# Row sums from a column of ones, context normalised in rows, and a gated output matrix, in an attention and expert layer

## The chip, the cores and the metric

The kernel runs on one core of one Trainium2 chip. The metric is device microseconds of one execution; lower is better. The numbers come from timed runs and from one profiled execution, whose rows are shown below. The engines are PE (TensorE; PEld its weight loads), DVE (VectorE), ACT (ScalarE), POOL (GpSimd) and SP (SyncE, which issues most transfers).

## The reference

The input is x of 16 batches x 256 positions x 128 channels in fp32. Six vectors per batch (shift, scale and gate, for attention and for the feed-forward part) come from a small product. With LN for the layer norm:

```
h = LN(x) * (1 + ca) + sa
Q, K, V = h @ Wq + bq, h @ Wk + bk, h @ Wv + bv        # 16 heads of 8
scores = Q K^T / sqrt(8) + Q . rel_table[clip(j - i)]
ctx = softmax(scores) V
x = x + ga * (ctx @ Wo + bo)
h = LN(x) * (1 + cb) + sb
x = x + gb * mixture of the 2 best of 8 experts(h)
```

Two facts let the kernel treat parts of this apart. The softmax's denominator may be applied after the product with V. And the gate ga differs by batch and channel only, so ga * (ctx @ Wo + bo) is ctx @ (Wo with its columns scaled by ga) plus the row ga * bo.

## The kernel before, in words

The attention stage is a hand-written pipeline over steps. A step (b, p) treats pair p (0 to 7, called slot p below) of heads of batch b: 128 steps in all. Every engine has a program of its own, in which `step(b, p)` is written out in order, and engines meet through counting semaphores only. In a step

- DVE takes the maxima (line 1312): four passes of 128x256 add the bias to the scores in psS and store the negated scores in NS and their extremes in nmax. It then takes the result of a job from psM (lines 1214 to 1236), copies the distances of six steps ahead from psDist to `stage` (line 1267, `put_out`), and takes the result of an extra job (line 1242).
- ACT computes four exponentials from NS to P (line 711). Each also sums its row into lsum (`accum_out`), which the profile shows as a second instruction, ACTIVATION_READ_ACCUMULATOR. Then ACT copies the turned P of the step before from psT to PT (line 722, `gather`).
- PE does, in this order: extra jobs of the slot; turn, eight transposes of P of the step before (line 968); scores of the next step, interleaved with the distances of six steps ahead (lines 950 and 956); a part of weigh, the product of PT with V into psO (line 984); and a job of the slot into psM.
- SP stores `stage` to DRAM and reads it back as `bias`, skewed.
- POOL prepares Q and K, the second layer norm and the rows for the experts.

Two tables set which jobs lie in which slot. `M_SLOTS` are jobs in psM: q23, k01, k23 in slots 0 to 2, logits and v in slot 3, y and nh in slot 4, u01, u23 and q01 in slots 5 to 7, each with a shift in batches. `X_SLOTS` are extra jobs in a spare part of psDist: rank, turn, back, tally (last batch), rows, and t in slots 1 to 6. `W_SLOTS` says which group of weigh stands where: group 0, both halves, in slot 4, and the last half of group 3 in slot 2 of the next batch. So the context of batch b-1 is completed in slots 0 to 4 of batch b:

1. Slot 0, DVE: `inverses` (line 1316) waits for all exponentials of the batch and takes the reciprocals of the 32 sums per row.
2. POOL: `widen` (line 565) repeats each reciprocal 8 times into linvD.
3. Slot 2, PE: `spread_l` (line 991) transposes linvD into the right half of psO. The left half holds the context, with the channels in the partitions.
4. Slot 3, ACT: `sums` (line 739) copies that half to lrow. DVE: `context` (line 1322) multiplies psO by lrow into ctxT.
5. Slot 4, PE: y (line 865) multiplies WoD by ctxT into psM; ACT applies the gate and the gated bias into yT (line 730), and t (line 902, slot 6) transposes yT back; DVE adds it to X (line 1247).

The columns of V are spread so that head c of group g lies in columns of its own: 32 columns per weight load, of which 8 hold values. psO is overwritten by the next batch's group 0, so weigh waits there for `ctx_done` (line 977).

After the attention stage the remaining jobs are closed, and the experts run over 39 tiles of 256 rows, with PE as the engine that is busy throughout; at the end results are weighed and stored.

Before the first step SP issues the loads one after the other: Wo and bv in four pieces each, then the rest of X, then 2 MB of zeros to DRAM.

The code of the functions that the change touches, with the line numbers of the profile:

## Time and profile before

| | |
|---|---|
| three runs | 685.5, 687.17 (median), 690.84 us |
| profiled execution | 685.29 us, its span 683.6 us |
| first maxima to the end of the last (128 steps) | 30.1 to 483.0 us of the span |
| busy in the span | PE 588.5, PEld 439.8, DVE 507.1, ACT 508.8, POOL 423.3 us |
| granted clock, mean | 0.96 of 2.4 GHz |

How to read it: the span runs from the first instruction to the last. A row of a timeline has the start in the span, the duration, the engine, the line in the code, the operation, output<-inputs, and the shapes; a bracket at its end is idle time of the engine before it and what ended it. Instructions overlap their neighbours, so the distance between two starts is what the first one costs its engine, and is less than its duration. Matmul rows are merged where they follow each other; x8 is their count. Idle time of an engine that others do not wait for costs nothing.

### The profile page before, as it was taken

To read this page: it belongs to the slowest core of one execution; us is meant where nothing else is said; L and a number is where in the kernel's file an instruction comes from. 1 tells how busy PE (TensorE), PEld (TensorE's weight loads), DVE (VectorE), ACT (ScalarE), POOL (GpSimd) and SP (SyncE) were. 2 spreads that over 40 slices of the span, in tenths; PEclk is the share of its full clock that TensorE was granted. 3 is DMA by queue.
4 is the path that set the end of the run, shared out by engine and by line. 5 is a ranking of instruction groups with operands and counts; after the bars stand their busy time and mean duration, and the time that the engine had idled before them with its cause. 6 is when DMAs were issued, how large, how long until landed. Compare 5 with 4: busy or idle time off the path is not lost. (4 is left out here: it accounts for less than half of the span.)

```text
span 683.6 us, 17706 instructions
## 1 busy us (share of the span) xinstructions
PE 588.5 (86%) x5108; PEld 439.8 (64%) x5108; DVE 507.1 (74%) x1888; ACT 508.8 (74%) x1578; POOL 423.3 (62%) x543
## 2 busy tenths in 40 slices
PE   5667789999899899899989989978798989999950
PEld 4444556666666566566666656655577979999940
DVE  6788988999999999999999999997565312222127
ACT  4157799999999999999989999998643434444434
POOL 2660655747668687686776966855366765554535
PEclk9777999999999999999999999999999999999975
DMA  5996678778787788778868878874525777565538
GB/s 142 308 230 202 198 235 248 228 235 248 214 245 241 213 252 246 228 219 260 249 208 242 252 213 247 243 236 148 189 82 174 236 234 228 198 217 185 176 97 274
DMA packets 173125, 149.03 MB, mean 218 GB/s; under 512 B 16182, under 2 KB 162642, under 8 KB 173030
## 3 DMA queue, kind: packets, MB, share of 16 engines
q1 hardware_dynamic: 168054, 139.33, 67.9%
q0 software_dynamic: 4544, 8.44, 3.7%
q8 instruction: 43, 0.70, 0.4%
q14 instruction: 52, 0.43, 0.2%
q10 hardware_dynamic: 432, 0.14, 0.1%
HBM read 83.71 MB, written 65.05 MB: 218 GB/s over the span
## 5 line engine op out<-in xcount | busy, mean ns | idle before, releaser
L711 ACT ACTIVATE P<-NS,nmax 128x256 f32<-128x256 f32 x512 | 254.2, 504 | 50.5 <-DVE nmax L1312 49.6
L1312 DVE CUSTOM_DVE_ANT_0 NS<-psS,bias 128x256 f32<-128x256 f32 x512 | 185.2, 417 | 2.3 <-PE psS L950 1.6
L968 PE MATMUL psT<-ident,P 128*128 128x128 f32 x1024 | 140.0, 281 | 8.9 <-ACT PT L722 8.8
L1267 DVE COPY stage<-psDist 128x768 f32<-128x768 f32 x125 | 118.1, 945 | 33.9 <-issue 25.2
L722 ACT ACTIVATE PT<-psT 128x512 f32<-128x512 f32 x256 | 136.4, 586 | 0.0
L968 PEld LDWEIGHTS psT<-ident,P 128*128 128x128 f32 x1024 | 118.2, 145 | 24.0 <-issue 9.8
L778 ACT ACTIVATE F<-psS,b1T 128x256 f32<-128x256 f32 x156 | 65.4, 471 | 86.5 <-PE psS L1061 86.5
L609 POOL DMA_INDIRECT results_d<-y,row_u x78 | 76.0, 974 | 56.7 <-DVE y L1458 40.8
L711 ACT ACTIVATION_READ_ACCUMULATOR P<-NS,nmax 128x1 f32 x512 | 100.3, 196 | 0.0
L950 PE MATMUL psS<-Kst,Qst 32*128 32x256 f32 x512 | 65.9, 336 | 34.7 <-DVE nmax L1312 29.9
L1061 PE MATMUL psS<-xT,w 128*128 128x256 f32 x312 | 80.6, 381 | 0.3 <-DMA w<-in_L_ffn_w_dram 0.3
L587 POOL TENSOR_TENSOR th<-z,th 128x512 f32<-128x512 f32 x28 | 35.7, 1277 | 70.8 <-ACT th L737 70.8
L601 POOL DMA_INDIRECT slots_d<-rows,slot_u x64 | 63.1, 987 | 26.4 <-issue 16.9
L984 PE MATMUL psO<-PT,V 128*32 128x256 f32 x1024 | 79.3, 394 | 0.0
L950 PEld LDWEIGHTS psS<-Kst,Qst 32*128 32x128 f32 x512 | 39.1, 189 | 62.2 <-DVE nmax L1312 52.0
L887 PE MATMUL psM<-hT,Wqk 128*128 128x256 f32 x244 | 70.1, 411 | 1.1 <-DVE z L1226 1.0
L956 PE MATMUL psDist<-Tst,Qst 32*128 32x192 f32 x488 | 58.2, 317 | 0.0
L887 PEld LDWEIGHTS psM<-hT,Wqk 128*128 128x128 f32 x244 | 43.1, 196 | 23.1 <-DVE xqk L1234 6.9
L1061 PEld LDWEIGHTS psS<-xT,w 128*128 128x128 f32 x312 | 53.4, 191 | 5.6 <-issue 1.0
L1458 DVE TENSOR_TENSOR y<-psO,b2R 128x256 f32<-128x256 f32 x19 | 8.1, 424 | 52.5 <-PE psO L1071 45.4
L1458 DVE TENSOR_TENSOR y<-psT,b2R 128x256 f32<-128x256 f32 x20 | 8.5, 425 | 51.8 <-PE psT L1071 47.8
L519 POOL TENSOR_TENSOR part<-xqk,lowQ 128x512 fp32r<-128x512 f32 x32 | 33.3, 1041 | 21.9 <-DVE xqk L1234 15.5
(254 smaller groups left out, 1044.2 us busy)
## 6 DMA issues: line engine op xcount, KB each, us to landing
dist_d<-stage SPq DMA_DIRECT2D x128, 384.0 KB, 3.0
bias<-dist_d SPq DMA_DIRECT2D x256, 192.0 KB, 3.3
w<-in_L_ffn_w_dram SPq DMA_DIRECT2D x39, 512.0 KB, 3.7
x<-slots_d SPq DMA_DIRECT2D x39, 129.0 KB, 3.0
y<-results_d SPq DMA_DIRECT2D x16, 256.0 KB, 5.0
dist_d<-zeros SPq DMA_DIRECT2D x1, 2048.0 KB, 14.4
out_dram<-y SPq DMA_DIRECT2D x8, 256.0 KB, 3.2
results_d<-y,row_u POOLq DMA_INDIRECT x78, 3.0
```

Source lines behind the costliest of these rows:

```text
L601: pool.indirect_dma_start(out=slots_d, out_offset=bass.IndirectOffsetOnAxis(ap=slot_u[:, j, n:n + 1], axis=0), in_=rows[:, j, r % RINGS, k ...
L609: pool.indirect_dma_start(out=results_d, out_offset=bass.IndirectOffsetOnAxis(ap=row_u[:, j, k:k + 1], axis=0), in_=y[:, j % HELD, k, :], ...
L711: act.activation(P[:, p % 2, h, q, :], NS[:, p % 2, h, q, :], ACT.Exp, scale=-1.0, bias=nmax[:, p % 2, k:k + 1], accum_out=lsum[:, b % 2, ...
L722: act.activation(PT[:, (p // 2) % 2, 2 * (p % 2) + h, :], psT[:, h, :], ACT.Copy)\
L778: i = act.activation(F[:, j % 2, k, :], psH[:, half, ET * n:ET * n + ET], ACT.Silu, bias=b1T[:, bass.ds(which[j], 1), k:k + 1].rearrange(" ...
L887: mm = pe.matmul(bank[:, S * n:S * n + S], w[:, 128 * g:128 * g + 128], hT[:], start=True, stop=True)
L950: mm = pe.matmul(psS[:, h, S * q:S * q + S], Qst[at, b % 2, g, 128 * q:128 * q + 128], Kst[at, b % 2, g, :], start=True, stop=True)
L968: mm = pe.transpose(psT[:, h, S * k + 128 * q:S * k + 128 * q + 128], P[:, p % 2, h, q, 128 * k:128 * k + 128], ident[:])
L984: mm = pe.matmul(psO[32 * a:32 * a + 32, 0:S], V[:, par, k, g, a, :, :].rearrange("p c d -> p (c d)"), PT[:, g % 2, a, S * k:S * k + S], s ...
L1061: mm = pe.matmul(psH[:, half, ET * n:ET * n + ET], w[:, j % DEEP, 0, at], xT[:, j % 2, :], start=True, stop=True)
L1267: dve.tensor_copy(stage[:, p % STAGES, :, :, :], bank[:, :, 0:2 * RW].rearrange("p h (q c) -> p h q c", q=2)).then_inc(dist_out, 1)
L1312: dve.tensor_tensor_reduce(NS[:, p % 2, h, q, :], psS[:, h, S * q:S * q + S], bias[:, p, h, q, :], 1.0, 3e38, ALU.add, ALU.min, nmax[:, p ...
```

## The change

The exponentials no longer sum their rows. V gets 16 columns per head instead of 8: eight values, a column of ones (written once), and seven of zeros; group g fills one half of psO (`g // 2`), so that psO's 512 columns hold, for each of 16 heads, eight values and the sum. The context of batch b-1 then goes another way:

1. Slot 3, ACT: `copy_values` copies all of psO to C. PE: `turn_values` transposes C back into psO in four pieces, with the positions in the partitions.
2. Slot 4, DVE: `context` takes the reciprocals of the 32 sums per row from psO and multiplies the values by them into ctx_r.
3. Slot 4, PE: ct transposes ctx_r into psM; ACT copies it to ctxT.
4. Slot 6, PE: y multiplies with ctxT as the stationary operand by WoG, and adds a product of a repeated column of the identity with gR, which gives every row the gated bias of the batch. DVE adds it to X.
5. Slot 7: gain. PE repeats the batch's gate row, DVE multiplies Wo by it into WoG. In batch 0, slot 4, gains turns all gates and gated biases into gR.

`inverses`, `widen`, `spread_l`, `sums` and t go. Wo and bv are reordered on the host, so that each is one transfer.

```diff
-           (("y", -1), ("nh", 2)), (("u01", -2),), (("u23", -2),), (("q01", 2),))
-X_SLOTS = ((), (("rank", -4),), (("turn", -2),), (("back", -2),), (("tally", 1 - B),), (("rows", -3),), (("t", -1),), ())
+           (("ct", -1), ("nh", 2)), (("u01", -2),), (("u23", -2),), (("q01", 2),))
+X_SLOTS = ((), (("rank", -4),), (("turn", -2),), (("back", -2),), (("gains", 0), ("tally", 1 - B)), (("rows", -3),),
+           (("y", -1),), (("gain", 0),))
...
-        V = early("V", [128, 2, JB, HG, 4, HG, D])
+        V = early("V", [128, 2, JB, HG, 4, 2, 2 * D])
...
-            for a in range(4):
-                at = slice(32 * a, 32 * a + 32)
-                sp.dma_start(WoD[at, :], Wo.rearrange("(g a d) e -> a g d e", a=4, d=D)[a]).then_inc(weights_in, 16)
-                sp.dma_start(bvT[at, :], bv.rearrange("(g a d x) -> a g d x", a=4, d=D, x=1)[a],
-                             allow_slow_non_contiguous=True).then_inc(weights_in, 16)
+            sp.dma_start(WoD[:], Wo).then_inc(weights_in, 16)
+            sp.dma_start(bvT[:], bv.rearrange("(e a) -> e a", a=1)).then_inc(weights_in, 16)
...
-                if b > 0:
-                    widen(b - 1)
...
                     act.activation(P[:, p % 2, h, q, :], NS[:, p % 2, h, q, :], ACT.Exp, scale=-1.0,
-                                   bias=nmax[:, p % 2, k:k + 1],
-                                   accum_out=lsum[:, b % 2, q, a, p // 2:p // 2 + 1]).then_inc(exp_done, 1)
+                                   bias=nmax[:, p % 2, k:k + 1]).then_inc(exp_done, 1)
...
-                    i = act.activation(yT[:], bank[:, 0:S], ACT.Identity, scale=modT[:, 2, b:b + 1],
-                                       bias=gabo[:, b:b + 1])
+                    i = act.activation(ctxT[:], bank[:, 0:S], ACT.Copy)
...
-            def sums(b):
-                act.wait_ge(ctx_full, b + 1)
-                past(act, ctx_done, b)
-                act.activation(lrow[:], psO[:, S:2 * S], ACT.Copy).then_inc(lrow_done, 1)
+            def copy_values(b):
+                act.wait_ge(values_done, HG * b + HG)
+                past(act, ctx_full, b)
+                act.activation(C[:], psO[:], ACT.Copy).then_inc(c_copied, 1)
...
-                elif name == "y":
+                elif name == "ct":
                     pe.wait_ge(ctx_done, b + 1)
-                    mm = pe.matmul(bank[:, 0:S], WoD[:], ctxT[:], start=True, stop=True)
+                    for k in range(2):
+                        mm = pe.transpose(bank[:, 128 * k:128 * k + 128], ctx_r[:, k, :], ident[:])
...
-                elif name == "t":
-                    pe.wait_ge(m_act, M_TAKEN["y", r][1])
+                elif name == "y":
+                    pe.wait_ge(m_act, M_TAKEN["ct", r][1])
+                    pe.wait_ge(x_dve, X_TAKEN["gain", r][0])
                     for k in range(2):
-                        mm = pe.transpose(spare[:, k, :], yT[:, 128 * k:128 * k + 128], ident[:])
+                        pe.matmul(spare[:, k, :], ctxT[:, 128 * k:128 * k + 128], WoG[:], start=True, stop=False)
+                        mm = pe.matmul(spare[:, k, :], ident[:, r:r + 1].broadcast_to([128, 128]), gR[:, 1, :],
+                                       start=False, stop=True)
...
+                elif name == "gain":
+                    mm = pe.matmul(spare[:, 0, :], ident[:, r:r + 1].broadcast_to([128, 128]), gR[:, 0, :],
+                                   start=True, stop=True)
...
-                        mm = pe.matmul(psO[32 * a:32 * a + 32, 0:S],
+                        mm = pe.matmul(psO[32 * a:32 * a + 32, S * (g // 2):S * (g // 2) + S],
...
-            def spread_l(b):
-                pe.wait_ge(linv_wide, b + 1)
+            def turn_values(b):
+                pe.wait_ge(c_copied, b + 1)
                 for q in range(2):
-                    mm = pe.transpose(psO[:, S + 128 * q:S + 128 * q + 128],
-                                      linvD[:, q, :, :, :].rearrange("p a g d -> p (a g d)"), ident[:])
+                    for r in range(2):
+                        mm = pe.transpose(psO[:, S * q + 128 * r:S * q + 128 * r + 128],
+                                          C[:, S * r + 128 * q:S * r + 128 * q + 128], ident[:])
                 mm.then_inc(ctx_full, 1)
...
-                    if p == 2:
-                        spread_l(b - 1)
+                if p == 3 and b > 0:
+                    turn_values(b - 1)
...
+                elif name == "gain":
+                    i = dve.tensor_tensor(WoG[:], WoD[:], spare[:, 0, :], ALU.mult)
...
+                values = psO[:].rearrange("p (n m d) -> p n m d", n=4, d=2 * D)
+                dve.wait_ge(ctx_full, b + 1)
+                dve.reciprocal(linv[:], values[:, :, :, D:D + 1].rearrange("p n m d -> p n (m d)")).then_inc(linv_done, 1)
                 if b > 0:
-                    dve.wait_ge(m_full, M_FULL["y", b - 1])
-                dve.tensor_tensor(ctxT[:], psO[:, 0:S], lrow[:], ALU.mult).then_inc(ctx_done, 1)
+                    dve.wait_ge(m_full, M_FULL["ct", b - 1])
+                dve.wait_ge(linv_done, b + 1)
+                dve.tensor_tensor(ctx_r[:].rearrange("p q (r m d) -> p (q r) m d", r=2, d=D), values[:, :, :, 0:D],
+                                  rep(linv[:], 3, D), ALU.mult).then_inc(ctx_done, 1)
...
-                if p == 0 and b > 0:
-                    inverses(b - 1)
...
-                if p == 3 and b > 0:
+                if p == 4 and b > 0:
                     context(b - 1)
```

What stands in a row on DVE in slot 4 of a batch, between the maxima of two slots (ISA rows are the maxima; the list counts lines of the changed kernel a little differently). Before:

```order
L1312 ISA nmax 128x1
L1229 TENSOR_SCALAR logitT<-psM,rb2T 128x256
L1222 COPY V<-psM 128x2x4x8 x4
L1267 COPY stage<-psDist 128x768
L1312 ISA NS,nmax<-psS,bias 128x256
```

With the change:

```order
L1316 ISA nmax 128x1
L1225 TENSOR_SCALAR logitT<-psM,rb2T 128x256
L1218 COPY V<-psM 128x2x4x8 x4
L1323 RECIPROCAL linv<-psO 128x32
L1327 TENSOR_TENSOR ctx_r<-psO,linv 128x256
L1268 COPY stage<-psDist 128x768
L1316 ISA NS,nmax<-psS,bias 128x256
```

The reciprocals and the context's product now stand between the copies of V and the copy to `stage`; before, they stood in slots 0 and 3.

What stands in a row on PE in slots 3 and 4 of a batch, from scores of slot 3 to turn of slot 5's extra jobs. Before:

```order
L881 MATMUL psM<-z,rw_s 32x256 x4
L881 MATMUL psM<-th,rw_s 32x256 x4
L861 MATMUL psM<-Wv_s,hT 128x128 x2
L968 MATMUL psT<-ident,P 128x128 x8
L950 MATMUL psS<-Kst,Qst 128x256 x2
L956 MATMUL psDist<-Tst,Qst 128x192 x2
L950 MATMUL psS<-Kst,Qst 128x256 x2
L956 MATMUL psDist<-Tst,Qst 128x192 x2
L984 MATMUL psO<-PT,V 32x256 x8
L865 MATMUL psM<-ctxT,WoD 128x256
L858 MATMUL psM<-ident,nrm 128x128 x2
L909 MATMUL psDist<-ident,logitT 128x128 x2
```

With the change:

```order
L990 MATMUL psO<-ident,C 128x128 x4
L865 MATMUL psM<-z,rw_s 32x256 x4
L865 MATMUL psM<-th,rw_s 32x256 x4
L844 MATMUL psM<-Wv_s,hT 128x128 x2
L962 MATMUL psT<-ident,P 128x128 x8
L944 MATMUL psS<-Kst,Qst 128x256 x2
L950 MATMUL psDist<-Tst,Qst 128x192 x2
L944 MATMUL psS<-Kst,Qst 128x256 x2
L950 MATMUL psDist<-Tst,Qst 128x192 x2
L979 MATMUL psO<-PT,V 32x256 x8
L849 MATMUL psM<-ident,ctx_r 128x128 x2
L841 MATMUL psM<-ident,nrm 128x128 x2
```

Four transposes of C have come in ahead of logits and v; y's product in slot 4 has become two transposes of ctx_r, and stands as before behind weigh of group 0 (psO<-PT,V x8).

What stands in a row on PE in slot 6, ahead of turn. Before, and with the change:

```order
L984 MATMUL psO<-PT,V 32x256 x4
L872 MATMUL psM<-h2T,rw_s 128x256 x2
L902 MATMUL psDist<-ident,yT 128x128 x2
L968 MATMUL psT<-ident,P 128x128 x8
L950 MATMUL psS<-Kst,Qst 128x256 x2
```

```order
L979 MATMUL psO<-PT,V 32x256 x4
L856 MATMUL psM<-h2T,rw_s 128x256 x2
L887 MATMUL psDist<-WoG,ctxT 128x128
L888 MATMUL psDist<-gR,ident 128x128
L887 MATMUL psDist<-WoG,ctxT 128x128
L888 MATMUL psDist<-gR,ident 128x128
L962 MATMUL psT<-ident,P 128x128 x8
```

In place of two transposes of yT there are four products ahead of turn and scores of that slot.

## Rows read from the trace of the kernel before

**Rows 1.** Busy us (count) by engine in batches 8 and 9, then clock, DMA share, GB/s
```profile
262.14:290.74 28.60, 25.99 (x253) 17.58 (x252) 27.13 (x102) 27.06 (x88) 21.00 (x28) 1.00 0.78 231
290.74:318.09 27.35, 25.77 (x255) 17.85 (x253) 25.46 (x98) 25.75 (x86) 20.50 (x28) 1.00 0.80 240
```

**Rows 2.** Groups by line, batches 1 to 14: count, busy us, mean ns, idle before
```profile
L1267 DVE COPY stage<-psDist 128x768 f32<-128x768 f32 x112 | 105.7, 944 | 24.2 <-issue 22.6 <-PE psDist L956 1.4
...
L711 ACT ACTIVATION_READ_ACCUMULATOR P<-NS,nmax 128x1 f32 x448 | 88.2, 197 | 0.0
```

**Rows 3.** Timeline of DVE, slots 4 to 6 of batch 9: start us, us, what
```profile
304.34 0.41 DVE L1312 CUSTOM_DVE_ANT_0 NS<-psS,bias 128x256 f32<-128x256 f32 x1
...
306.11 0.60 DVE L1222 COPY V<-psM 128x64 f32<-128x64 f32 x4
306.64 0.94 DVE L1267 COPY stage<-psDist 128x768 f32<-128x768 f32 x1
307.50 0.41 DVE L1312 CUSTOM_DVE_ANT_0 NS<-psS,bias 128x256 f32<-128x256 f32 x1
...
309.86 0.96 DVE L1267 COPY stage<-psDist 128x768 f32<-128x768 f32 x1 [0.91 <-issue]
...
310.87 0.41 DVE L1312 CUSTOM_DVE_ANT_0 NS<-psS,bias 128x256 f32<-128x256 f32 x1
```

**Rows 4.** Timeline of PE, slots 4 to 6 of batch 9
```profile
305.85 0.38 PE L950 MATMUL psS<-Kst,Qst 32*128 32x256 f32 x2
...
306.28 1.07 PE L984 MATMUL psO<-PT,V 128*32 128x256 f32 x16
307.28 0.70 PE L865 MATMUL psM<-ctxT,WoD 128*128 128x256 f32 x2
307.82 0.38 PE L858 MATMUL psM<-ident,nrm 128*128 128x128 f32 x2
...
308.25 1.04 PE L968 MATMUL psT<-ident,P 128*128 128x128 f32 x8
309.22 0.38 PE L950 MATMUL psS<-Kst,Qst 32*128 32x256 f32 x2
...
311.19 0.38 PE L902 MATMUL psDist<-ident,yT 128*128 128x128 f32 x2
311.84 1.11 PE L968 MATMUL psT<-ident,P 128*128 128x128 f32 x8 [0.27 <-ACT PT L722]
312.88 0.39 PE L950 MATMUL psS<-Kst,Qst 32*128 32x256 f32 x2
```

**Rows 5.** Timelines: DVE slot 0, DVE slot 3; PE even slot 6, slots 0 and 3
```profile
292.72 0.34 DVE L1320 RECIPROCAL linv<-lsum 128x32 f32<-128x32 f32 x1
292.98 0.90 DVE L1267 COPY stage<-psDist 128x768 f32<-128x768 f32 x1
...
303.15 0.41 DVE L1326 TENSOR_TENSOR ctxT<-psO,lrow 128x256 f32<-128x256 f32 x1
303.48 0.94 DVE L1267 COPY stage<-psDist 128x768 f32<-128x768 f32 x1
...
284.30 0.38 PE L950 MATMUL psS<-Kst,Qst 32*128 32x256 f32 x2 [0.63 <-DVE nmax L1312]
...
292.26 0.39 PE L950 MATMUL psS<-Kst,Qst 32*128 32x256 f32 x2 [0.52 <-DVE nmax L1312]
...
302.68 0.39 PE L950 MATMUL psS<-Kst,Qst 32*128 32x256 f32 x2
```

**Rows 6.** Timeline of ACT, exponentials of slot 5 of batch 9
```profile
309.15 0.50 ACT L711 ACTIVATE P<-NS,nmax 128x256 f32<-128x256 f32 x1
309.55 0.20 ACT L711 ACTIVATION_READ_ACCUMULATOR P<-NS,nmax 128x1 f32 x1
309.64 0.50 ACT L711 ACTIVATE P<-NS,nmax 128x256 f32<-128x256 f32 x1
```

**Rows 7.** Timeline of DVE at the start, a copy to stage
```profile
26.47 0.96 DVE L1267 COPY stage<-psDist 128x768 f32<-128x768 f32 x1 [2.12 <-DMA dist_d<-stage]
```

More of the change, by code:

```diff
@@ L73, in list_jobs @@
                     if 0 <= b + shift < B and (name != "rank" or (b + shift) % 2)
-                    and (name != "tally" or b == B - 1)]
+                    and (name != "tally" or b == B - 1) and (name != "gains" or b == 0)]
             done[b, p] = full, dve, act
@@ L750, in step @@
                 if p == 3 and b > 0:
-                    sums(b - 1)
+                    copy_values(b - 1)
                 for name, of in M_OF.get(at, ()):
@@ L803, in _ @@
             act.activation(p1[:, 0:1], ident[:, 0:1], ACT.Silu)
-            sums(B - 1)
-            act.wait_ge(m_full, M_FULL["y", B - 1])
-            take("y", B - 1, banks[1])
+            copy_values(B - 1)
+            act.wait_ge(m_full, M_FULL["ct", B - 1])
+            take("ct", B - 1, banks[1])
             units(0, 1)
@@ L979, in weigh @@
                         pe.wait_ge(job_done, START + 1)
+                        pe.wait_ge(ones_in, 1)
                     else:
@@ L1113, in _ @@
             closing(0)
-            spread_l(B - 1)
+            turn_values(B - 1)
             turn_x(0)
@@ L1297, in _ @@
             dve.wait_ge(v_zero, 1)
+            for g in range(HG):
+                i = dve.memset(V[:, :, :, g, :, g % 2, D:D + 1].rearrange("p b k a d -> p (b k) (a d)"), 1.0)
+            i.then_inc(ones_in, 1)
             first("v", 5, 0, psO)
```

65 lines of the change are left out of this document (29 added, 36 removed).

## The prediction

> **What bounds the kernel now.** I read the busy times by stretch first, then the groups by line, then the timeline of single engines, batch by batch. Between the first batch and the last, one batch takes 28.60 us (even batches, which also choose experts) or 27.35 us (odd ones), and in it three engines are busy almost all the time: in batch 9 PE 25.77, DVE 25.46 and ACT 25.75 of 27.35 us, at a granted clock of 1.00 [rows 1]. A busy share cannot tell which of the three sets the pace, so I looked at which one waits. DVE's idle time stands before one group, the copy of the distances to `stage` (line 1267), 24.2 us in 112 copies [rows 2]. That copy needs distances that PE computes inside scores of the next step, and these wait for the end of this step's maxima (line 1312). So there is a loop: maxima on DVE, scores on PE, copy on DVE, next maxima. Its times in batch 9: maxima of slot 4 start at 304.34 and scores at 305.85, 1.51 later; scores of slot 5 start at 309.22 and the copy at 309.86, 0.64 later; a copy lasts 0.86 to the next maxima (306.64 to 307.50) [rows 3, 4]. A slot can thus not be shorter than 1.51 + 0.64 + 0.86 = 3.01 us, plus what DVE does behind the copy. ACT appears in this loop only through PE: turn (line 968) is queued ahead of scores and waits for ACT's copy to PT. In the slots shown that wait ends one gap, 0.27 us in slot 6 [rows 4].
>
> **The exponentials without their sums.** 512 reads of the accumulator go; 448 of them lie in this stretch, 197 ns each [rows 2]. They overlap: an exponential starts at 309.15, its read at 309.55 and the next exponential at 309.64 [rows 6]. So one read costs the engine 0.09 us, 32 x 0.09 = 2.9 us per batch. In the loop this is worth only the places where turn waits for ACT: slot 6 of an odd batch, where scores start at 312.88 although the maxima began at 310.87 and would allow 312.38 [rows 3, 4], 0.50 us; and an estimated 0.07 us in slot 1 of even batches. In an even batch scores of slot 6 wait 0.63 us for DVE, not for ACT [rows 5]. ACT's wider copy of psO (512 columns in place of 256) and the narrower work on ct are hidden behind that slack.
>
> **The context moves to slot 4.** Now the reciprocal stands in slot 0 and the product in slot 3, each just ahead of a stage copy that has to wait for scores anyway. Slot 0: the reciprocal starts at 292.72, scores at 292.26, so the copy could start at 292.90 and starts at 292.98; removing it gives back 0.08, not 0.26. Slot 3: product at 303.15, scores at 302.68, copy possible at 303.32 and made at 303.48; that gives back 0.16 [rows 5].
> In slot 4 both stand behind the copies of V, where there was no wait: the copy to stage starts at 306.64, 2.30 after the maxima [rows 3]. There the reciprocal takes 0.34 (its row now, 128x32) and ends at 2.64; the product has to wait for it, at least 0.03, and takes 0.41 as the product now does [rows 5]: 2.67 to 3.08. The copy follows 0.33 after the product's start, at 3.00. No row shows the two on psO with its stride; each may cost 0.13 (the spacing of the V copies, four in 0.60 [rows 3]) up to 0.60; I take today's rows, the nearest of the same shape.
> The second effect is larger. weigh of the new batch (line 984, both halves of group 0) overwrites psO and waits for `ctx_done`. Before, the product was done a slot earlier and weigh started at 306.28, 1.94 after the maxima [rows 4]; in the changed kernel it starts at 3.08 + 0.05 (an estimate for the release) = 3.13, 1.19 later. Behind it on PE stand ct, nh, rows, turn and scores of slot 5, and on these waits DVE's next copy. ct, two transposes at an estimated 0.27 (0.11 each and a start), stands in for y's product, 0.54 (307.28 to 307.82 [rows 4]). So scores of slot 5 come 1.19 - 0.27 = 0.92 later, counted from the maxima of slot 4. DVE itself loses only 0.70, but it waits for these scores: **+0.92 us per batch** over slots 4 and 5.
>
> **PE's new work.** turn_values puts four transposes where two were (0.11 each by the spacing in turn: eight in 1.04, the last 0.27 [rows 4]) into slot 3, 0.4 us more there. Scores of slot 4 come up to 0.5 late by it; the copy in slot 4 is at 3.00 only, so this stays hidden. y is four fp32 products; one product is two instructions, as y's row now shows (x2), so eight at the spacing of 0.11, 0.88 us in slot 6 where t's two transposes took 0.22 (311.19, and turn could follow at 311.41 but for its wait [rows 4]). Odd batches: from scores of slot 5 to those of slot 6 it is 312.88 - 309.22 = 3.66 now, ACT's wait included; then 1.97 up to where t stands (309.22 to 311.19), 0.88 for y and 0.97 for turn (308.25 to 309.22) give 3.82: **+0.16** [rows 4], and ACT's relief is spent. Even batches: PE has 0.63 of slack there [rows 5], so 0. Were y free, odd batches would win 0.50.
> gain, a 128x128 product in DVE's slot 7 behind the copy, has no cover: between 0.13 and 0.33 (the spacing of the 256-column product [rows 5]), **+0.20**.
>
> **Sum.** Odd: 0.92 + 0.16 + 0.20 - 0.16 - 0.08 = +1.04. Even: 0.92 + 0.20 - 0.16 - 0.08 - 0.07 = +0.81. Seven of each, batches 1 to 14: +13.0 us. Batch 0 has gain, gains and ones, +0.5. The last batch has no V and no stage copies after slot 1, and DVE's planning fills it: 0. Start: ten small transfers on SP (Wv, bo, and Wo and bv in four pieces each) become four, and the 2 MB of zeros behind them go out earlier, behind which the first stores of `stage` may queue; a `stage` copy of the start waits 2.12 us for such a store [rows 7]. Bounds -2.5 (all of it and the next copy's share) and +0.5 (the wait is the store's own, and the ones cost DVE four instructions); I take -1.2. In the tail POOL's widening goes and PE gets 0.6 more: 0. Together +12.3 on the profiled execution's 685.29 us (span 683.6 and 1.7 around it): 697.6. The median of the three runs shown is 687.17, 1.9 more, so 699.5.
>
> **Rivals.**
> *ACT sets the pace.* For it: ACT is as busy as any engine. The Trainium skill, "Perfetto Trace Analysis", section Identifying the Most-Contended Engine, tells to find the bound by occupancy for the vector and scalar engines and to improve that one first; by it ACT, ahead of DVE in batch 9, is the right engine to relieve. Against it: ACT's waits in the rows above. If true, the pace falls to DVE's busy time with 0.3 of new work: 25.46 + 0.3 for 27.35 and 27.13 + 0.3 for 28.60 [rows 1], 1.4 us per batch, 14 x 1.4 = 19.6 less: about 667.
> *Given back.* The stall is there, but PE's slack behind slot 5 (0.63 in even batches [rows 5]) and ACT's 0.50 in odd ones absorb most, if y overlaps with turn's wait: +0.2 per batch, about 690.
> *The clock.* PE waits 0.7 us more in slot 4; if its granted clock falls to the lower level, 1.2 GHz, for some microseconds in each batch (it is 1.00 in both rows now [rows 1]), PE's 5 us around it cost some 1.5 more: 14 x 1.5 = 21, about 720.
>
> **Chances.** Forecast 0.62, ACT 0.13, given back 0.17, clock 0.08. A change of 1% is about what a measurement of this kernel tells from none (680 to 694). The forecast's own range is 693 to 706, from 0.13 or 0.60 for the two context instructions and the start's bounds. For 8 in 10: 683 to 707. Faster by over 1% 0.15, within 1% 0.19, slower 0.66.
>
> **What would show it.** Right: weigh of group 0 starts 3.1 us after the maxima of slot 4, its idle time put down to ctx_r; the stage copy of slot 5 still has an idle gap of about 0.9 or more; the reads of the accumulator are gone and ACT's busy time in a batch falls by some 3 us without the batch getting shorter; a batch lasts 28.4 and 29.4 us. Wrong: batches at 26 us with DVE without gaps (ACT paced), or slots 4 and 5 no longer than 6.5 us together in an odd batch.

## The result, and the profile after

The changed kernel takes 697.26 us (median of 4 runs, 696.53 to 699.99) beside 686.34 us of the kernel before (683.55 to 690.84): 1.016 of it, interval 1.0097 to 1.0223, 10.9 us. A second measurement, in the last group of experiments, gave 699.84 beside 685.33: 1.022, interval 1.0176 to 1.0270. It is slower, by about what was forecast. But the terms behind the sum are not all as forecast, and one thing that nobody looked for, VectorE (DVE) meeting GpSimd (POOL), is in the sum with both signs.

The page of the changed kernel's profile, its first lines, and busy times by stretch for batches 8 and 9 (columns as in [rows 1]):

```profile
span 698.3 us, 17512 instructions
...
PE 604.8 (87%) x5270; PEld 461.6 (66%) x5270; DVE 515.6 (74%) x1909; ACT 468.6 (67%) x1066; POOL 416.9 (60%) x528
```

```profile
262.97:292.83 29.86, 26.89 (x264) 18.89 (x263) 27.90 (x104) 24.11 (x55) 20.45 (x27) 1.00 0.75 221
292.83:321.48 28.65, 26.63 (x265) 18.98 (x264) 26.02 (x97) 23.69 (x54) 20.15 (x27) 1.00 0.78 230
```

Beside [rows 1]: ACT works 2.95 us less in an even batch and 2.06 less in an odd one, and the batches are 1.26 and 1.30 us longer. The granted clock is 1.00 in both. In the groups by line of batches 1 to 14 the reads of the accumulator are gone, and the idle time before the copy to `stage` has grown from 24.2 us [rows 2] to 30.0:

```profile
L698 ACT ACTIVATE P<-NS,nmax 128x256 f32<-128x256 f32 x448 | 191.1, 499 | 50.5 <-DVE nmax L1316 37.8 <-PE psT L962 12.7
...
L1268 DVE COPY stage<-psDist 128x768 f32<-128x768 f32 x112 | 106.7, 953 | 30.0 <-issue 26.4
```

The timeline of DVE in slots 4 to 6 of batch 9, answering to [rows 3]:

```profile
306.31 0.41 DVE L1316 CUSTOM_DVE_ANT_0 NS<-psS,bias 128x256 f32<-128x256 f32 x1
...
308.61 0.34 DVE L1323 RECIPROCAL linv<-psO 128x32 f32<-128x32 f32 x1
309.05 0.42 DVE L1327 TENSOR_TENSOR ctx_r<-psO,linv 128x256 f32<-128x256 f32 x1
309.39 0.95 DVE L1268 COPY stage<-psDist 128x768 f32<-128x768 f32 x1
310.26 0.41 DVE L1316 CUSTOM_DVE_ANT_0 NS<-psS,bias 128x256 f32<-128x256 f32 x1
...
312.90 0.96 DVE L1268 COPY stage<-psDist 128x768 f32<-128x768 f32 x1 [1.18 <-issue]
...
313.91 0.41 DVE L1316 CUSTOM_DVE_ANT_0 NS<-psS,bias 128x256 f32<-128x256 f32 x1
```

And PE there, answering to [rows 4]:

```profile
309.58 1.07 PE L979 MATMUL psO<-PT,V 128*32 128x256 f32 x16 [0.75 <-ACT PT L708]
310.58 0.44 PE L849 MATMUL psM<-ident,ctx_r 128*128 128x128 f32 x2
310.86 0.38 PE L841 MATMUL psM<-ident,nrm 128*128 128x128 f32 x2
...
312.26 0.38 PE L944 MATMUL psS<-Kst,Qst 32*128 32x256 f32 x2
...
314.23 0.38 PE L887 MATMUL psDist<-WoG,ctxT 128*128 128x128 f32 x2
...
315.12 1.04 PE L962 MATMUL psT<-ident,P 128*128 128x128 f32 x8
316.08 0.39 PE L944 MATMUL psS<-Kst,Qst 32*128 32x256 f32 x2
```

weigh of group 0 starts at 309.58, 3.27 after the maxima of slot 4 (1.94 before). The row puts its wait down to ACT's copy to PT, and not to ctx_r as the prediction expected; that copy ended at about the same time as the product (309.05 + 0.42 = 309.47). But it is of a later slot than the PT that group 0 reads (in the kernel before it only starts at 306.85, behind weigh at 306.28), and the run with the context first, below, shows that the product was what weigh waited for. Scores of slot 5 start 5.95 after those maxima (4.88 before), and the copy to stage of slot 5 waits 1.18 instead of 0.91.

The length of each slot, from one start of the maxima to the next, in two steady batches (us; the forecast is the prediction's difference):

| slot | odd: before, after | difference | even: before, after | difference | forecast |
|---|---|---|---|---|---|
| 0 | 3.05, 3.02 | -0.03 | 3.05, 3.03 | -0.02 | -0.08 |
| 1 and 2 | 7.38, 7.44 | +0.06 | 6.70, 6.63 | -0.07 | 0 odd, -0.07 even |
| 3 | 3.17, 3.02 | -0.15 | 3.17, 3.03 | -0.14 | -0.16 |
| 4 and 5 | 6.53, 7.60 | +1.07 | 7.73, 8.13 | +0.40 | +0.92 |
| 6 | 3.86, 4.02 | +0.16 | 4.17, 5.05 | +0.88 | +0.16 odd, 0 even |
| 7 | 3.36, 3.55 | +0.19 | 3.78, 3.99 | +0.21 | +0.20 |
| batch | 27.35, 28.65 | +1.30 | 28.60, 29.86 | +1.26 | +1.04 odd, +0.81 even |

Odd batches follow the forecast slot by slot. Even ones reach nearly the same sum in another way: less in slots 4 and 5, and 0.88 in slot 6, where nothing was expected. The timelines of DVE and POOL at those two places show why. In slot 5 of batch 8, before and after:

```profile
281.32 1.27 POOL L521 TENSOR_TENSOR Kst<-xqk,part 128x512 fp32r<-128x512 f32 x1
...
281.77 1.09 DVE L1347 TENSOR_TENSOR ahead_of<-logit 128x256 f32<-128x256 f32 x1
...
282.53 0.60 POOL L591 COPY rows<-rows 128x256 f32<-128x256 f32 x1
```

```profile
281.58 1.28 POOL L519 TENSOR_TENSOR Kst<-xqk,part 128x512 fp32r<-128x512 f32 x1
...
282.81 0.39 POOL L584 COPY rows<-rows 128x256 f32<-128x256 f32 x1
...
283.44 0.42 DVE L1349 TENSOR_TENSOR ahead_of<-logit 128x256 f32<-128x256 f32 x1
```

And at the end of slot 6, before and after:

```profile
286.83 0.21 DVE L1356 TENSOR_TENSOR chosen<-place,places 128x64 f32<-128x64 f32 x1
286.94 1.27 POOL L587 TENSOR_TENSOR th<-z,th 128x512 f32<-128x512 f32 x1 [3.69 <-ACT th L737]
```

```profile
287.57 1.27 POOL L580 TENSOR_TENSOR th<-z,th 128x512 f32<-128x512 f32 x1 [4.24 <-ACT th L722]
...
287.83 1.09 DVE L1358 TENSOR_TENSOR chosen<-place,places 128x64 f32<-128x64 f32 x1
...
288.84 0.41 DVE L1316 CUSTOM_DVE_ANT_0 NS<-psS,bias 128x256 f32<-128x256 f32 x1
```

`ahead_of` and `chosen` are small instructions of the expert choice, with all operands in SBUF. Alone they last 0.42 and 0.21. Where POOL is already in a product on SBUF when they start, they last 1.09 and end a little behind POOL's product (it ends at 281.32 + 1.27 = 282.59, `ahead_of` at 282.86; at 287.57 + 1.27 = 288.84, `chosen` at 288.92). Before, `ahead_of` is caught, in slot 5; after, it starts 1.86 behind Kst's product and is free, and `chosen` is caught instead: 0.67 less in slot 5, 0.88 more in slot 6. So 1.07 - 0.67 = 0.40 is the even batches' row of slots 4 and 5, and the 0.88 of slot 6 is this one instruction. Batches 4 and 14 bear it out: in batch 4 of the kernel before `ahead_of` is free (0.43), and with the change slots 4 and 5 are 1.07 longer, as in odd batches, and the batch 1.91; in batch 14 it lasts 0.56 before, and they are 0.92 and 1.78 longer. The Trainium skill, "SBUF — State Buffer", section Who interferes with whom, has the rule: VectorE with two inputs in SBUF and GpSimd reading SBUF share a port pair, the one that is issued first has it for its whole instruction, and the other stands still. By that rule DVE loses what is left of POOL's instruction, 0.82 and 1.01 us here; the rows agree but for 0.13 to 0.15: it loses 0.67 and 0.88. They show the other side too: POOL's copy rows, which starts within the caught `ahead_of`, lasts 0.60, and 0.39 where `ahead_of` is not beside it.

Why `chosen` is caught now: it starts 4.04 after the maxima of slot 6 in both kernels, but POOL's product waits for ACT's tanh, and ACT's four exponentials are 4 x 0.09 shorter without their reads. POOL starts 3.78 instead of 4.15 after the maxima (287.57 - 283.79 and 286.94 - 282.79). The relief of ACT moved POOL across the start of `chosen`.

Outside the steady batches the profiled executions give: first maxima at 27.1 us instead of 30.1; batch 0 35.4 instead of 38.9; batches 1 to 14 together 405.6 instead of 388.8, 16.8 more; the last batch 26.0 instead of 25.1; and behind it 204.2 instead of 200.6. The sum is 14.7, the difference of the spans. (The profiled execution took 699.99 us, the longest of the four.)

### The profile page after: what moved, and what is told of

Same layout as the page of the kernel before. It is cut to its first block and busy times, and to the rows that moved or that the text cites. A ratio compares the mean times of both kernels' runs of the same rounds, so it can differ in the third digit from the quotient of the medians.

```text
span 698.3 us, 17512 instructions
## 1 busy us (share of the span) xinstructions
PE 604.8 (87%) x5270; PEld 461.6 (66%) x5270; DVE 515.6 (74%) x1909; ACT 468.6 (67%) x1066; POOL 416.9 (60%) x528
## 5 line engine op out<-in xcount | busy, mean ns | idle before, releaser
L698 ACT ACTIVATE P<-NS,nmax 128x256 f32<-128x256 f32 x512 | 218.4, 499 | 81.0 <-DVE nmax L1316 68.3
L962 PE MATMUL psT<-ident,P 128*128 128x128 f32 x1024 | 137.5, 279 | 0.5 <-ACT PT L708 0.5
L962 PEld LDWEIGHTS psT<-ident,P 128*128 128x128 f32 x1024 | 120.7, 145 | 5.2 <-ACT P L698 1.4
L944 PEld LDWEIGHTS psS<-Kst,Qst 32*128 32x128 f32 x512 | 38.9, 188 | 57.1 <-DVE nmax L1316 47.4
L1067 PE MATMUL psT<-w,F 128*128 128x128 f32 x320 | 42.9, 278 | 0.1
```

The lines of the kernel that those rows point to most:

```text
L698: act.activation(P[:, p % 2, h, q, :], NS[:, p % 2, h, q, :], ACT.Exp, scale=-1.0, bias=nmax[:, p % 2, k:k + 1]).then_inc(exp_done, 1)
L944: mm = pe.matmul(psS[:, h, S * q:S * q + S], Qst[at, b % 2, g, 128 * q:128 * q + 128], Kst[at, b % 2, g, :], start=True, stop=True)
L962: mm = pe.transpose(psT[:, h, S * k + 128 * q:S * k + 128 * q + 128], P[:, p % 2, h, q, 128 * k:128 * k + 128], ident[:])
L1067: mm = pe.matmul(psY[j % 2][:, 128 * i:128 * i + 128], F[:, j % 2, k, 128 * i:128 * i + 128], w[:, j % DEEP, 1, 128 * k:128 * k + 128], st ...
```

## The experiments

All are beside runs of the kernel before on the same chip; ratios are to those. Batch lengths are of steady batches in each run's profile.

**1. ACT's relief alone**, on the kernel before:

```diff
-                                   bias=nmax[:, p % 2, k:k + 1],
-                                   accum_out=lsum[:, b % 2, q, a, p // 2:p // 2 + 1]).then_inc(exp_done, 1)
+                                   bias=nmax[:, p % 2, k:k + 1]).then_inc(exp_done, 1)
+            pool.memset(lsum[:], 256.0)
```

> The kernel before with one thing taken away: the exponentials no longer write their sums (the tile of sums is filled once with 256 instead, so the context is scaled by that constant and not by its row's sum; all other work stays). It is the relief of ACT alone, without any of the change's other parts. The theory of the prediction (the loop maxima, scores, stage copy sets the pace and ACT is waited for in slot 6 of odd batches and a little in slot 1 of even ones): 0.50 us per odd batch and 0.07 per even one, seven of each, 4 us less than before, 0.994 of it; ACT's busy time falls by some 40 us all the same. Rival, ACT sets the pace: 1.4 us or more per batch, 20 us or more, 0.97 of before or less.

Measured: 689.97 us, 1.0051 of before, interval 1.0022 to 1.0080: slower, against both. ACT's busy time fell from 508.8 to 468.0 us. Odd batches went from 27.34 to 26.98, by slot 6 (3.86 to 3.50; batch 5 alone came at 27.56, by its slot 0); even ones from 28.60 to 29.47, by slot 6 (4.17 to 5.06). Batches 1 to 14 together are 2.6 longer in the profile. DVE and POOL there:

```profile
286.71 1.27 POOL L588 TENSOR_TENSOR th<-z,th 128x512 f32<-128x512 f32 x1 [3.32 <-ACT th L736]
286.96 1.10 DVE L1355 TENSOR_TENSOR chosen<-place,places 128x64 f32<-128x64 f32 x1
```

The collision comes with the relief alone, without any other part of the change.

**2. The sums back**, on the changed kernel:

```diff
-                                   bias=nmax[:, p % 2, k:k + 1]).then_inc(exp_done, 1)
+                                   bias=nmax[:, p % 2, k:k + 1],
+                                   accum_out=lsum[:, p % 2, k:k + 1]).then_inc(exp_done, 1)
```

> The changed kernel with the sums of the exponentials written again, to a tile that nobody reads: ACT gets back its 512 reads, nothing else differs. Theory (ACT has slack again in slots 4 and 7, and is waited for in slots 5 and 6 of odd batches alone, where it works without a gap): 0.5 us per odd batch, 3 to 4 us in all over the changed kernel's 697, so about 700.5. Rival, ACT is no longer waited for anywhere: no difference, 697. Rival, ACT sets the changed kernel's pace: 14 x 2.9 = 40 us more.

Measured: 694.05 us, 1.0104 (1.0068 to 1.0140), where the changed kernel has 1.016 and 1.022: if anything faster for 512 reads more. All three expectations missed it. Even batches fall from 29.86 to 28.98, in slot 6 alone (5.05 to 4.18):

```profile
285.64 0.21 DVE L1360 TENSOR_TENSOR chosen<-place,places 128x64 f32<-128x64 f32 x1
285.75 1.28 POOL L581 TENSOR_TENSOR th<-z,th 128x512 f32<-128x512 f32 x1 [4.63 <-ACT th L724]
```

`chosen` starts 0.11 before POOL and is free. Odd batches came at 28.18 instead of 28.65, which is not the reads: it is slot 2 alone, where `slot_u`, a conversion on DVE, lasts 0.16 and not 0.6 as in the first profile of the changed kernel; experiment 12 shows that this varies by itself. Slot 6 of odd batches did not move (4.02 and 4.03), and no other slot grew: ACT is waited for nowhere in the changed kernel.

**3. The context ahead of the copies of V** (DVE's order in slot 4):

```diff
-                if p == 4 and b > 0:
-                    context(b - 1)
                 link_up(1)
...
+                if p == 4 and b > 0:
+                    context(b - 1)
                 at = before(b, p)
```

> The changed kernel with DVE's reciprocal and context product ahead of the copies of logits and V in slot 4, straight behind the maxima, instead of behind them; no work is added or taken away. Theory (the stall that counts is PE's: weigh of group 0 waits for the product, and through it the scores of slot 5 and DVE's copy to stage): weigh starts some 2.3 us after the maxima of slot 4 instead of 3.27, the gap of 1.18 before the stage copy of slot 5 shrinks to 0.2 or 0.3, 0.9 per batch, 13 us less than the changed kernel, about 684. Rival, DVE's own added work in slot 4 is what costs: its order there changes nothing, 697. Rival in between, the late copy of V then holds ct on PE (it shares the bank): 0.3 per batch, about 693.

Measured: 692.52 us, 1.0078 (1.0046 to 1.0109). Slot 5 of odd batches went from 3.65 to 3.15, of even ones from 4.18 to 3.80; slot 4 stayed at 3.95. That is half of the 0.9 that was expected. (Odd batches fell from 28.65 to 27.70; the other 0.47 is `slot_u` in slot 2, as in experiment 2, and not the edit.) PE and DVE in batch 9 (maxima of slot 4 at 307.34):

```profile
309.79 1.07 PE L979 MATMUL psO<-PT,V 128*32 128x256 f32 x16
310.79 0.44 PE L849 MATMUL psM<-ident,ctx_r 128*128 128x128 f32 x2
...
312.80 0.39 PE L944 MATMUL psS<-Kst,Qst 32*128 32x256 f32 x2
```

```profile
311.29 0.41 DVE L1316 CUSTOM_DVE_ANT_0 NS<-psS,bias 128x256 f32<-128x256 f32 x1
...
313.44 0.96 DVE L1268 COPY stage<-psDist 128x768 f32<-128x768 f32 x1 [0.69 <-issue]
```

weigh runs straight behind the scores at 309.79, 2.45 after the maxima, with no wait: it was the product that held it. But scores of slot 5 now start 1.51 after the maxima of slot 5 (311.29 to 312.80), the loop's own time. These maxima come late by DVE's 0.79 in slot 4, which the order cannot remove. Of the loss in slots 4 and 5, 0.5 was PE's wait and 0.57 is DVE's work (3.95 + 3.15 against 6.53). The total is near the number of the rival in between, 693, but not by its mechanism: ct starts 1.00 behind weigh, as in the first profile (310.58 - 309.58), so it does not wait for the copy of V.

**4. `chosen` moved**, on the changed kernel:

```diff
-... (6, 1): (3,), (6, 2): (4,), (7, 0): (5, 6), ...
+... (6, 1): (3,), (7, 0): (4, 5, 6), ...
```

> The changed kernel with one instruction of DVE's expert choice (chosen, both operands in SBUF) moved from the end of slot 6 to slot 7 of the even batches. In the profile of the changed kernel it lasts 1.09 us there and ends where a product of POOL's on SBUF ends, while it takes 0.21 in the kernel before. Theory (it stands in a collision with POOL, which the change moved from slot 5, where PE's slack took up part of it, into slot 6, where nothing does): 0.87 us less in each of the six even batches from 4 to 14, 5 us less than the changed kernel, about 692. Rival, PE sets the length of slot 6 in even batches (y's four products): no difference, 697.

Measured: 694.66 us, 1.0106 (1.0065 to 1.0147). Slot 6 of even batches 5.05 to 4.05, slot 7 3.99 to 4.24 (`chosen` lasts 0.20 there): 0.75 per even batch, six of them 4.5 us; the total is 2.6 and 5.2 under the two measurements of the changed kernel. The rival falls. And slot 6 at 4.05 is the 4.17 of before less the 0.13 that `chosen` takes there: y's four products cost even batches nothing.

**5. The transfers of the start alone**, on the kernel before:

```diff
-            for a in range(4):
-                at = slice(32 * a, 32 * a + 32)
-                sp.dma_start(WoD[at, :], Wo.rearrange("(g a d) e -> a g d e", a=4, d=D)[a]).then_inc(weights_in, 16)
-                sp.dma_start(bvT[at, :], ...)
+            sp.dma_start(WoD[:], Wo).then_inc(weights_in, 16)
+            sp.dma_start(bvT[:], bv.rearrange("(e a) -> e a", a=1)).then_inc(weights_in, 16)
```

> The kernel before with one part of the change alone: Wo and bv are put in the order of the tiles ahead of the launch, and eight small transfers become two (all else as before). Theory after the first profiles: SP's own issuing is what the eight transfers cost, 4.09 to 9.61 us, against 4.11 to 5.06 in the changed kernel; the zeros go out 4.8 us earlier, at 6.1 instead of 11.0, and the first stage stores behind them by as much; the first maxima start at 27.1 to 28.5 us instead of 30.1, and the total falls by 3 to 5 us, to 0.994 of before. Rival, the step of the prediction: 1.2 us less (at most 2.5), 0.998. Rival, the loads of the start hide it: no difference.

Measured: 684.11 us, 0.9958 (0.9927 to 0.9988), 3.2 us less; first maxima at 27.1. Steady batches as before (28.59 and 27.33). The timeline of SP's queue in the kernel before, and in the changed one:

```profile
4.09 0.82 SPq L409 DMA_DIRECT2D WoD<-in_L_attn_Wo_dram  x1
4.95 0.63 SPq L410 DMA_DIRECT2D bvT<-in_L_attn_bv_dram  x1
...
10.12 0.81 SPq L412 DMA_DIRECT2D X<-in_L_attn_q_dram  x1
10.97 4.43 SPq L414 DMA_DIRECT2D dist_d<-zeros  x1
```

```profile
4.11 0.43 SPq L408 DMA_DIRECT2D WoD<-in_L_attn_Wo_dram  x1
4.58 0.43 SPq L409 DMA_DIRECT2D bvT<-in_L_attn_bv_dram  x1
5.23 0.87 SPq L410 DMA_DIRECT2D X<-in_L_attn_q_dram  x1
6.14 4.69 SPq L412 DMA_DIRECT2D dist_d<-zeros  x1
```

It is SP's issuing that costs: eight small pieces hold the next transfer, the rest of X, back until 10.12, two whole ones until 5.23, and the zeros go out 4.83 earlier. Which of the two, X or the zeros, the first maxima gain from was not tried.

**6. The two instructions moved**, on the kernel before:

```diff
-... (5, 2): (0,), (6, 0): (1, 2), (6, 1): (3,), (6, 2): (4,), (7, 0): (5, 6), ...
+... (6, 0): (0, 1, 2), (6, 1): (3,), (7, 0): (4, 5, 6), ...
```

> The kernel before with two instructions of DVE's expert choice moved in the even batches: ahead_of (both operands in SBUF, 1.09 us at the end of slot 5, where it ends with POOL's product to Kst) goes to the head of the chain in slot 6, and chosen goes from slot 6 to slot 7; no work is added or taken away. Theory (a DVE instruction with all its operands in SBUF that starts while POOL works ends only with POOL's instruction, and DVE's length of the slot decides there): ahead_of takes 0.42 again, slot 5 falls from 4.57 to about 3.4, slot 6 stays at about 4.2, slot 7 grows by 0.1 to 0.2: 0.8 us or more in each of six even batches, 5 us less than before, 0.993. Rival, PE's scores end last in slots 5 and 6 and cover the collision: no difference.

Measured: 681.76 us, 0.9948 (0.9922 to 0.9973), 5.6 us less. Slot 5 of even batches 4.57 to 3.37, slot 6 4.17 to 4.50, slot 7 3.79 to 4.04; `ahead_of` lasts 0.42 in all of them. Only batches 6, 8, 10 and 12 had the collision with Kst's product, and each falls by 0.62 (28.60 to 27.98), so the steady batches account for 2.5 us; the rest of the 5.6 is not in them and stays open (the interval goes down to 1.9 us).

**7. ACT's relief without the collision**: the edits of 1 and 6 together.

> The kernel before without the sums of the exponentials (filled once with 256, as before in this study: the context is scaled by that constant) and with the two moved instructions: ACT's relief without the collision that it brought in slot 6 (chosen then meets POOL's product behind the tanh). Theory (the relief by itself is worth a little, the collision took more than it gave): 0.25 us per odd batch and some 0.4 per even one below the kernel with the moved instructions alone, 3 to 5 us, about 677, where the relief without the move is 690. Rival, the loss in the run without sums has another cause than the collision: about 690 less the 5 us that the move alone brings, 685. Rival, ACT sets the pace: below 667.

Measured: 679.23 us, 0.9894 (0.9865 to 0.9922), and 27.9 and 27.0 us per even and odd batch. Under experiment 6, in the same group of runs, that is 2.5 us. With the two instructions out of POOL's way the relief of ACT gives a little, by slot 6 of odd batches (3.86 to 3.50); even batches gain 0.06, not the expected 0.4. With the two in POOL's way it took 3.5 us.

**8. y halved**, on the changed kernel:

```diff
-                        pe.matmul(spare[:, k, :], ctxT[:, 128 * k:128 * k + 128], WoG[:], start=True, stop=False)
-                        mm = pe.matmul(spare[:, k, :], ident[:, r:r + 1].broadcast_to([128, 128]), gR[:, 1, :],
-                                       start=False, stop=True)
+                        mm = pe.matmul(spare[:, k, :], ctxT[:, 128 * k:128 * k + 128], WoG[:], start=True, stop=True)
```

> The changed kernel with y made of two products instead of four: the two that add the gated bias are left out (so that part is missing from the result). The step of the prediction (y's eight instructions on PE end last before turn in odd batches, and each 0.11 of them counts): 0.44 us less per odd batch, 3 us in all, about 694. Rival, from the profile of the changed kernel (y ends at 315.12 and turn's exponentials of ACT come at 315.07, so turn would wait for ACT instead; in even batches scores start 0.13 later than the maxima allow): 0.05 per odd and 0.13 per even batch, 1 us or no difference that can be measured, 696 to 697.

Measured: 696.25 us, 1.0134 (1.0102 to 1.0167). The total lies in the rival's range and, beside two measurements of the changed kernel 2.6 apart, settles nothing. The profile decides for the step of the prediction and against the rival: slot 6 of odd batches falls from 4.02 to 3.58, the 0.44 of four instructions at 0.11, and that of even ones stays at 5.06. PE in batch 9: turn starts 0.45 behind y's start, where it was 315.12 - 314.23 = 0.89:

```profile
315.91 0.61 PE L887 MATMUL psDist<-WoG,ctxT 128*128 128x128 f32 x4
316.36 1.04 PE L960 MATMUL psT<-ident,P 128*128 128x128 f32 x8
317.32 0.39 PE L942 MATMUL psS<-Kst,Qst 32*128 32x256 f32 x2
```

**9. Both repairs of the changed kernel**: the edits of 3 and 6 together.

> The changed kernel with both repairs: the context ahead of the copies of logits and V in slot 4, and ahead_of and chosen moved in the even batches. If the batch's loss is made of PE's wait in slot 4, the collision in slot 6, and DVE's own 0.79 in slot 4 that neither removes: odd batches 27.8 us (as with the context first alone), even ones 28.3 to 28.5, about 12 us less over batches 4 to 14 than the changed kernel, a total near the kernel before (0.995 to 1.002 of it) in spite of a start that is 3 us shorter. Rival, the two parts cover each other: 29 us or more per even batch, 1.005 or more.

Measured: 686.02 us, 1.0024 (0.9994 to 1.0054): as before, just above the expected 0.995 to 1.002, and no better, though its start is shorter. Even batches last 28.54, slots 4 and 5 7.11 in both kinds of batch and slot 6 of even ones 4.50, so the two parts do not cover each other. Odd batches came at 28.15 in four of five (`slot_u` lasts 0.62 there) and at the expected 27.70 in the one where it lasts 0.16.

**10. The kernel before with the start and the moved instructions**: the edits of 5 and 6 together.

> The kernel before with the two transfers at the start (Wo and bv put in order ahead of the launch) and the two moved instructions. Each alone gave 3 and 5 to 6 us in other parts of the kernel; if they add up, 8 to 9 us less than before, 678 to 679, 0.987 of it. Rival, a start that is 3 us shorter is given back in the first batch, whose length changes from one execution to the next: 0.994 as with the moved instructions alone.

Measured: 679.77 us, 0.9925 (0.9902 to 0.9949), 5.6 us less. It beats both kernels. The product of the two alone, 0.9958 x 0.9948 = 0.9906, lies in the interval, and so does the rival's 0.994; the expected 0.987 does not. Steady batches are those of experiment 6 (27.99 and 27.34); first maxima at 27.9, batch 0 38.6. So the profile has 2.2 us of the start and 2.5 of the steady batches, 4.7: both parts are there, and the expectation counted all of experiment 6's 5.6, of which the batches show 2.5.

**11. The stall alone**, on the kernel before: the product moves to slot 4, the reciprocal stays.

```diff
-                if p == 3 and b > 0:
+                if p == 4 and b > 0:
                     context(b - 1)
```

> The kernel before with one thing moved: the context's product on DVE from slot 3 to slot 4, behind the copies of V (reciprocal, sums and everything else stay). It is the stall of the change alone. Theory (weigh of group 0 waits for the product, and the scores of slot 5 and DVE's copy behind it): weigh starts 2.30 + 0.41 + 0.10 = 2.8 us after the maxima of slot 4 instead of 1.94, slots 4 and 5 of an odd batch together 0.8 to 0.9 us longer, slot 3 0.15 shorter: 0.7 per odd batch, as much or less in even ones (there the collision of ahead_of with POOL may change too), 8 to 10 us more than before, 1.012 to 1.015. Rival, only DVE's own work counts: 0.33 in slot 4 less 0.15 in slot 3, 2.5 us, 1.004.

Measured: 692.27 us, 1.0101 (1.0069 to 1.0133), a little under the range. Odd batches are 0.72 longer (slot 3 -0.15, slots 4 and 5 +0.87). PE in batch 9 (maxima of slot 4 at 307.46): weigh at 2.81, scores of slot 5 at 5.75 instead of 4.88.

```profile
310.27 1.07 PE L984 MATMUL psO<-PT,V 128*32 128x256 f32 x16 [0.70 <-issue]
...
313.21 0.38 PE L950 MATMUL psS<-Kst,Qst 32*128 32x256 f32 x2
```

Steady even batches are only 0.06 longer (0.33 in batch 12). There the later copy to stage has moved `ahead_of` to where a short copy of POOL's starts instead of beside Kst's product: 0.43 instead of 1.09, as in the changed kernel, and POOL's copy lasts 0.67 instead of 0.40. In batch 12, where the two start at the same time, it is `ahead_of` that lasts 0.68.

```profile
284.50 1.28 POOL L521 TENSOR_TENSOR Kst<-xqk,part 128x512 fp32r<-128x512 f32 x1
...
285.71 0.43 DVE L1347 TENSOR_TENSOR ahead_of<-logit 128x256 f32<-128x256 f32 x1
285.72 0.67 POOL L591 COPY rows<-rows 128x256 f32<-128x256 f32 x1
```

**12. The changed kernel again.**

> The changed kernel once more, as it is, beside the kernels that are compared with it. It was 697.26 us, 1.016 of before with an interval of 1.010 to 1.022; its steady batches 28.64 and 29.86 us. If the copy that converts slot_u in slot 2 of odd batches meets POOL's product by chance of a hundredth of a microsecond (2.10 and 2.10 in the profile), odd batches may come at 28.2 in this profile instead; the total then reads 3 us less.

Measured: 699.84 us, 1.0223 (1.0176 to 1.0270). `slot_u` did vary: 0.62 in two of five odd batches and 0.16 in three (0.61 to 0.63 in all five of the first profile), and odd batches average 28.4; but the total did not read less. In all five `slot_u` starts 0.01 to 0.02 us behind a product of POOL's (nrm<-X,mv). First maxima at 27.8, batch 0 38.6, and 201.6 us behind the last batch, where the first profile has 35.4 and 204.2.

## Why the prediction was right, and where its terms were not

Right in its forecast: 699.5 stood beside 697.26 and 699.84, slower, and in odd batches by the mechanism that it named. In even batches the sum is near the forecast by two collisions that nobody foresaw, and that the total came so close is in part luck: terms too low in the batches stand against terms too high at the start.

**What bounds it.** The loop of maxima, scores and copy is shown by experiment 3: with PE's wait gone, scores stand 1.51 behind the maxima, as the prediction had it. ACT's rival fell three times: 41 us less of ACT's work made the kernel before slower (experiment 1), gave 2.5 us at best (7), and put back it did no harm (2). The step "ACT's relief is worth 0.50 in slot 6 of odd batches, 0.07 in slot 1 of even ones" measured 0.36 and 0.07 (experiment 1): four exponentials without their reads end 4 x 0.09 sooner, which is less than the wait of 0.50. The Trainium skill, "Perfetto Trace Analysis", section Identifying the Most-Contended Engine, would begin with the engine of the highest occupancy, and 25.75 of 27.35 us [rows 1] spoke for ACT; the measurement does not agree, and the waits before an engine's instructions, not its busy share, told what it was worth.

**Slots 0, 3 and 7** (forecast -0.08, -0.16, +0.20) measured -0.02, -0.15 and +0.20.

**Slots 4 and 5** (+0.92): +1.07 in odd batches. The mechanism was right, a size was off: the product starts 0.44 after the reciprocal's start instead of 0.37 (a gap of 0.10 where 0.03 was put), and weigh 0.11 behind the product's end instead of 0.05, which makes 3.27 of the forecast's 3.13. ct took 0.28 for the estimated 0.27. Experiment 11 gives the stall with the product alone, 0.87, of weigh 0.87 later.

**Slot 6** (+0.16 odd, 0 even): +0.16 odd, and experiment 8 confirms its working (0.11 for each of y's instructions). In even batches the step that failed is "PE has 0.63 of slack there, so 0". PE's slack was real (experiment 4). But the step took DVE's work in that slot as given, as if a duration in one profile belonged to the instruction: `chosen` was 0.21 before and is 1.09 now. And it took ACT's earlier end as worth something or nothing, and did not ask what a faster ACT starts sooner. Experiments 1, 2 and 4 show it from three sides: ACT's relief alone brings the collision, ACT's reads put back remove it, moving `chosen` removes it.

**The sum over batches 1 to 14** was +13.0; it is +16.8 in the profile. A steady odd batch has 0.26 more than forecast, 0.15 of it the stall; an even one 0.45 more, 0.15 for the stall and 0.88 - 0.67 = 0.21 for the two collisions. Batches 4 and 14, where `ahead_of` was not caught by Kst's product before, have 1.1 and 1.0 more. Batches 1 to 3 have 1.2 less, all of it in batch 1, whose length changes from profile to profile (28.0 to 29.8 us) for no reason that a run shows.

**The start** (-1.2, bounds -2.5 to +0.5) is mis-sized, and by another mechanism: -3.0 in the first profile, which is the far end of what nine profiles with the shorter start give (first maxima at 27.1 to 28.5 us, 27.8 in the middle, where five with the old one have 30.1 to 30.3, so some -2.4); -3.2 in the times of experiment 5, with an interval from -0.8 to -5.0. The prediction priced the wait of one stage copy behind a store [rows 7]; what counts is SP, which spends 0.62 us or more on each of the eight pieces. It was one view away: SP's queue at the start shows it.

**Batch 0 and the tail** were not terms of any weight. Batch 0 was 3.5 shorter in the first profile; that is no effect of the change, since it comes at 34.4 to 35.4 or at 38.3 to 39.2 us in profiles of either kind (34.9 in experiment 6 with the old start, 38.6 in experiment 12 with the new one). What decides it stays open. PE's granted clock differs there from one execution to the next (0.77 over the 38.9 us of the first profile of before, 0.86 over the 34.9 of experiment 6, with the same start), but it alone does not decide: it is 0.82 over the 35.4 of the first profile of the changed kernel and over the 38.6 of experiment 12. The tail's +3.6 goes with the clock: behind the last batch PE's work takes 175.5 us before, where the clock stays at 1.00 until PE is done, and 179.8 after, where it falls twice on the way, some 40 and some 78 us behind the last batch; in experiment 12, the same kernel, it falls once, PE takes 176.0 and the tail 201.6.

**The other rivals.** The clock in the batches did not fall: it is 1.00 throughout batches 1 to 14 of the changed kernel. "Given back" did not happen by its mechanism: slots 4 and 5 of an odd batch are 7.60 together, and what even batches had less there, 0.67, is `ahead_of` and not PE's slack.

The errors ran against each other: in the first profile 3.8 more in the batches, 1.8 less at the start.

## What to carry to other kernels

A duration on VectorE need not be the instruction's own where GpSimd works at the same time: look up each small SBUF-only instruction at the places that set a slot's length, and compare it with the same instruction in another batch. When an engine with slack is made faster, ask which engine it releases sooner, and what that one then stands in the way of. And move a dependent step only to a place that waits anyway: the context's two instructions cost 0.17 us per batch where the stage copy behind them was late in any case (slots 0 and 3), and 1.07 where no wait stood.

## What the runs showed of the hardware that was not expected

VectorE and GpSimd. All of `ahead_of`, `chosen` and the conversion `slot_u` (to integers, in slot 2 of odd batches) show the same: 0.42, 0.21 and 0.16 alone, about 1.09, 1.09 and 0.60 where POOL's product had begun. With POOL 0.25 ahead of `chosen` (experiment 1) the price is 0.89, with POOL 0.11 behind (experiment 2) it is nothing; for `slot_u` in experiment 12, hundredths of a microsecond separate the two. POOL pays in its turn: its copy rows lasts 0.60 to 0.67 instead of 0.40 where `ahead_of` has begun. The waiting stands in the profile as duration, not as idle time, so no view of waits shows it. A reduction is not affected: `slot_f` lasts 0.21 in the middle of POOL's product to Qst in the changed kernel (batch 9: it starts at 300.69, POOL works from 300.17 to 301.46).

TensorE's clock. Some 38 us behind the last batch PE waits about 2.5 us for the last expert choice in both kernels. Behind that wait the granted clock stayed at 1.00 in the profile of before and fell for some 3.4 us in that of the changed kernel. Busy times by stretch there, before and after (columns as in [rows 1]):

```profile
522.00:525.00 3.00, 1.25 (x9) 1.23 (x10) 2.54 (x13) 0.00 (x0) 0.85 (x3) 1.00 0.33 121
525.00:528.00 3.00, 3.00 (x23) 2.80 (x22) 0.95 (x6) 1.42 (x4) 2.04 (x3) 1.00 0.26 44
```

```profile
533.10:536.10 3.00, 1.78 (x9) 1.63 (x10) 2.26 (x13) 0.00 (x0) 0.95 (x4) 0.80 0.19 71
536.10:539.10 3.00, 3.00 (x14) 2.77 (x13) 0.00 (x0) 0.84 (x2) 2.39 (x3) 0.63 0.13 44
```

The means 0.80 and 0.63 are of the two levels, 2.4 and 1.2 GHz: 1.2 and 2.2 us of the two stretches at the lower one. In 3 us at 0.63 PE begins 14 instructions where it begins 23 at 1.00. With nearly the same wait it fell in the profiles of experiments 1, 3, 4, 7, 8, 9, 11 and 12 and not in those of 2, 5, 6 and 10; what decides it was not tried.
